# A four-stage decoder block on one core: FFN weights prepared early, experts' products reordered, and scratch for squares with split value products in the grouped attention

## The reference

```python
h = x + L0_xattn(x, mask, ctx, ...)     # 4 batch rows of 256 tokens, width 256;
                                        # keys = 1601 rows of ctx + 256 own; one head of 256
h = h + L0_ffn(h)                       # 32 experts of 96 + 16 chunk experts of 128, top 4 by
                                        # sigmoid gate, weights renormalised
h = h + L1_xattn(h, ctx)                # 16 query heads, 4 key heads of 128, 1601 keys,
                                        # RMS norm of q and k
out = h + L1_ffn(h)                     # BitNet: y = down(rms(silu(gate(q)) * up(q)) quantised)
# L1_ffn: q = clip(round(x * 127 / max|x|), -128, 127)      per token
#         w = clip(round(w / mean|w|), -1, 1) * mean|w|     per matrix: gate, up 1024x256, down 256x1024
```

## Time and profile before

| what | value |
|---|---|
| median of 3 runs | 1772.55 us (1770.74 to 1777.56) |
| profiled execution, its span | 1774.77 us, 1773.0 us |
| PE, busy | 1471.0 us (83%) |
| DVE, busy | 1182.2 us (67%) |
| ACT, busy | 991.8 us (56%) |
| POOL, busy | 561.8 us (32%) |

### The profile page before, as it was taken

The page is one execution under the profiler, slowest core; times in us unless marked ns, Lnnn a source line. Parts: engine busy times, 40 slices in busy tenths (PEclk is TensorE's granted clock), DMA queues, the critical chain, the costliest instruction groups (busy, mean ns, idle before and its releaser), DMA issues. The chain is left out here.

```text
span 1773.0 us, 26328 instructions
## 1 busy us (share of the span) xinstructions
PE 1471.0 (83%) x9411; PEld 1328.1 (75%) x9414; DVE 1182.2 (67%) x2432; ACT 991.8 (56%) x2068; POOL 561.8 (32%) x458
## 2 busy tenths in 40 slices
PE   5787737888847889899999989999989999999835
PEld 4777636787736788888888878888878888888723
DVE  3444367898755776677667667667666766767577
ACT  3333215788624555566556565665656665656455
POOL 2101224454253422334233243232324322322124
PEclk9888957999978999999999999999999999999968
DMA  2011017899711202011010110110201101000020
GB/s 91 32 37 37 19 55 255 295 301 324 237 56 51 51 19 65 19 36 39 7 39 19 53 49 7 39 31 15 65 19 37 39 7 40 19 10 22 21 83 25
DMA packets 80673, 118.19 MB, mean 67 GB/s; under 512 B 16676, under 2 KB 61896, under 8 KB 80552
## 3 DMA queue, kind: packets, MB, share of 16 engines
q1 hardware_dynamic: 75992, 104.14, 18.0%
q0 software_dynamic: 4560, 12.46, 3.1%
HBM read 106.14 MB, written 10.42 MB: 66 GB/s over the span
## 5 line engine op out<-in xcount | busy, mean ns | idle before, releaser
L1617 ACT ACTIVATE ga_pT<-ga_ps_t 128x512 fp32r<-128x512 f32 (+1 forms) x512 | 243.7, 516 | 217.0 <-PE ga_ps_t L1850 216.7
L1747 DVE TENSOR_TENSOR ga_pT<-ga_ps_t,ga_pT 128x512 fp32r<-128x512 f32 (+1 forms) x512 | 278.0, 581 | 46.9 <-ACT ga_pT L1617 45.4
L1625 ACT ACTIVATE ga_probs<-ga_ps_s,ga_neg_max 128x1200 f32<-128x1200 f32 (+1 forms) x256 | 235.4, 927 | 110.6 <-DVE ga_neg_max L1768 110.5
L1850 PE MATMUL ga_ps_t<-all_eye,ga_probs 128*128 128x128 f32 (+1 forms) x1664 | 228.0, 274 | 14.9 <-DVE ga_pT L1747 8.2
L1850 PEld LDWEIGHTS ga_ps_t<-all_eye,ga_probs 128*128 128x128 f32 (+1 forms) x1664 | 194.3, 141 | 29.7 <-DVE ga_pT L1747 10.1
L1763 DVE TENSOR_REDUCE ga_part_max<-ga_ps_s 128x1 f32<-128x1200 f32 x128 | 178.7, 1396 | 10.0 <-PE ga_ps_s L1801 9.4
L1801 PE MATMUL ga_ps_t<-side_w_kv,side_encT 128*128 128x256 f32 (+1 forms) x1170 | 161.2, 287 | 27.6 <-DVE side_kn L1740 22.6
L1801 PEld LDWEIGHTS ga_ps_t<-side_w_kv,side_encT 128*128 128x128 f32 (+1 forms) x1170 | 144.8, 185 | 39.6 <-DVE side_kn L1740 29.2
L1888 PE MATMUL ga_ps_m<-ga_pT,side_v 128*128 128x512 f32 (+1 forms) x416 | 161.0, 423 | 13.7 <-DVE ga_out_n L1781 13.4
L1527 POOL TENSOR_TENSOR ga_oT<-ga_out_n,ga_oT 128x256 fp32r<-128x256 f32 x64 | 47.4, 741 | 352.2 <-ACT ga_oT L1640 352.2
L1801 PE MATMUL ga_ps_s<-side_kT,ga_qT 128*128 128x400 f32 (+1 forms) x768 | 157.1, 354 | 1.9 <-ACT ga_probs L1625 1.6
(11 more groups left out here) (305 smaller groups left out, 3054.5 us busy)
## 6 DMA issues: line engine op xcount, KB each, us to landing
ex_raw<-in_L_ffn_packed SPq DMA_DIRECT2D x63, 704.0 KB
ga_w_raw<-in_L_xattn_Wq SPq DMA_DIRECT2D x16, 512.0 KB
ga_w_raw<-in_L_xattn_Wo SPq DMA_DIRECT2D x16, 512.0 KB, 4.7
ga_inv_rows<-ga_inv_row SPq DMA_DIRECT2D x64, 128.0 KB
mix_y_rows<-ex_y SPq DMA_DIRECT2D x63, 128.0 KB
ca_cache<-in_ctx SPq DMA_DIRECT2D x4, 1536.0 KB
side_enc<-in_ctx_turned SPq DMA_DIRECT2D x12, 512.0 KB, 5.3
side_w_kv_raw<-in_L_xattn_Wk SPq DMA_DIRECT2D x16, 128.0 KB
```

The source lines that it names most:

```text
L1617: nc.scalar.activation(dst(HI), src, ACT.Copy, scale=scale).then_inc(read, 1)
L1625: nc.scalar.activation(dst, src, ACT.Exp, bias=neg_max[:, n % 2:n % 2 + 1], accum_out=half_sum[:, n % 4, k:k + 1]).then_inc(exped, 1)
L1747: nc.vector.tensor_tensor(dst(LO), src, f32(dst(HI)), ALU.subtract).then_inc(empty, 1)
L1850: mm = nc.tensor.transpose(out[0:top, i * P:(i + 1) * P], probs[step % PB][:, tile * P:tile * P + top], eye[:, :])
```

## The change

Six edits:

1. **FFN weights early.** The host lays the three FFN matrices turned (`ffn_turned`, 128 x 3 x 2048). In `cached_attention` SP loads them behind the first cache load, ACT sums absolute values in rounds 0 to 2, and in the last round PE, DVE and ACT make mean, clip and sign. SP stores 1.5 MB of bf16 signs to DRAM and waits for that. `bit_ffn` loads them ready (3 x 0.5 MB), has no preparation left, and takes the token norm in two parts (tiles 0 to 1, then 2 to 7).
2. The loops of `cached_attention` are written out.
3. **Experts:** on PE the gate/up product of block `i-1` stands before the transposes of block `i`; on ACT `silu` before the copy of `xT`; on DVE `a` before the low part of `xT`. Wq of group 0 is loaded here already.
4. **Start of the grouped attention:** Wq's split comes first, its low part on DVE, `norm` comes before `k_eps` on POOL, a one-element `Exp` runs at the start, and the splits of group 1's Wq, Wk/Wv and of Wo move from before step 0 to steps 0, 2 and 4. Group 1's `q` and `qT` jobs move to steps 2, 3 and 5.
5. **Squares** go to `squares_of` (two halves in turn for `kv`, both for `q`).
6. **Value products** of a step are cut into two pieces; the first late job stands between them.

```diff
@@ cached_attention, ACT and DVE, in a round (b < 3, and last)
+                if b < W:
+                    act.wait_ge(f_in, 16 * W)
+                    nc.scalar.activation(f_sign[:, b, :], f_raw[:, b, :], ACT.Abs, accum_out=f_abs[:, b:b + 1]
+                                         ).then_inc(f_summed, 1)
...
+                    for n in range(W):
+                        nc.vector.tensor_scalar(f_raw[:, n, :], f_raw[:, n, :], f_scale[:, n:n + 1], 1.0, ALU.mult, ALU.min
+                                                ).then_inc(f_step, 1)
+                        dve.wait_ge(f_step, n + 3)
+                        nc.vector.tensor_scalar(f_raw[:, n, :], f_raw[:, n, :], -1.0, ROUND, ALU.max, ALU.add
+                                                ).then_inc(f_rounded, 1)
@@ cached_attention, SP
+            sp.wait_ge(f_signed, W)
+            sp.dma_start(ternary.rows, f_sign[:, :, :]).then_inc(f_stored, 16)
+            sp.wait_ge(f_stored, 16)
@@ grouped_attention, the plan
         if to == 1:
-            early, late = [], [e for e in late if e[0] in ("q", "q_eps", "qT")]
+            early, late = [], {2: [("q", 0, 1)], 3: [("q", 1, 1), ("q_eps", 0, 1)],
+                               5: [("qT", 0, 1), ("qT", 1, 1)]}.get(s, [])
...
-        return (([("scores", 0, n)] if n < N else []) + turns[0:2] + early + weighed(n) + late[:1] + turns[2:4]
-                + late[1:])
+        return (([("scores", 0, n)] if n < N else []) + turns[0:2] + early + values[0:1] + late[:1] + values[1:2]
+                + turns[2:4] + late[1:])
@@ grouped_attention, ACT
                 elif kind == "kv":
-
                     at, top, src = kv_view(e)
-                    nc.scalar.activation(kn[0:top, at, :], src[:, :, 0, :], ACT.Square)
-                    nc.scalar.activation(v[g % 2][0:top, HI, at, :], src[:, :, 1, :], ACT.Copy).then_inc(read, 1)
+                    nc.scalar.activation(v[g % 2][0:top, HI, at, :], src[:, :, 1, :], ACT.Copy)
+                    nc.scalar.activation(squares_of[0:top, nth % 2, 0:at.stop - at.start, :], src[:, :, 0, :], ACT.Square
+                                         ).then_inc(read, 1)
...
+            split_q(0)
+            nc.scalar.activation(warm[:, :], half_power[:, 0:1], ACT.Exp)
             for e in prologue:
-                if e[0] == "xT":
-                    split_q(0)
                 if e[0] in RING:
                     ring(e)
-            split_out(0)
-            split_q(1)
-            split_kv(2)
@@ grouped_attention, DVE
+                if kind == "kv":
+                    at, top, src = kv_view(e)
+                    dve.wait_ge(*copied(e))
+                    nc.vector.tensor_copy(kn[0:top, at, :], src[:, :, 0, :])
+                    nc.vector.tensor_tensor(v[g % 2][0:top, LO, at, :], src[:, :, 1, :],
+                                            f32(v[g % 2][0:top, HI, at, :]), ALU.subtract).then_inc(empty, 1)
+                    nc.vector.tensor_reduce(k_sq[0:top, at], squares_of[0:top, nth_squared[e] % 2, 0:at.stop - at.start, :],
+                                            AX.X, ALU.add).then_inc(squares, 1)
+                    return
```

More of the change, by code:

```diff
@@ L160, in cached_attention @@
         added = counted("added", QT, before=1)
+        f_in = sem("f_in")
+        f_summed = sem("f_summed")
+        f_mean = sem("f_mean")
+        f_step = sem("f_step")
+        f_rounded = sem("f_rounded")
+        f_signed = sem("f_signed")
+        f_stored = sem("f_stored")
         block = ctx.enter_context(nc.Block())
         def rounds(eng, body):
-            with eng.Fori(0, B - 1) as b:
-                body(b, False)
-            body(B - 1, True)
+            for b in range(B):
+                body(b, b == B - 1)
         @block.sync
@@ L183, in _ @@
             load_cache(kv_cache[0:1, :, :])
-            with sp.Fori(0, B - 1) as b:
-                row = kv_cache[bass.ds(b + 1, 1), :, :]
+            for n in range(W):
+                sp.dma_start(f_raw[:, n, :], ffn_turned[:, n, :]).then_inc(f_in, 16)
+            for b in range(B - 1):
                 sp.wait_ge(v_lo.sem, v_lo.level(b, 1))
-                load_cache(row)
+                load_cache(kv_cache[b + 1:b + 2, :, :])
+            sp.wait_ge(f_signed, W)
+            sp.dma_start(ternary.rows, f_sign[:, :, :]).then_inc(f_stored, 16)
+            sp.wait_ge(f_stored, 16)
         @block.gpsimd
@@ L256, in body @@
                     move(m)
+                if b < W:
+                    act.wait_ge(f_in, 16 * W)
+                    nc.scalar.activation(f_sign[:, b, :], f_raw[:, b, :], ACT.Abs, accum_out=f_abs[:, b:b + 1]
+                                         ).then_inc(f_summed, 1)
+                if last:
+                    for n in range(W):
+                        act.wait_ge(f_rounded, n + 1)
+                        nc.scalar.activation(f_sign[:, n, :], f_raw[:, n, :], ACT.Copy, bias=-ROUND
+                                             ).then_inc(f_signed, 1)
                 move_hi(ready.level(b, M_TURNS + 1 if last else M), *output)
@@ L456, in body @@
                         turn(m, b + 1)
+                    if last and i == SHARE:
+                        pe.wait_ge(cleared, 4)
+                        pe.wait_ge(f_summed, W)
+                        nc.tensor.matmul(ps_t[:, 0, 0:W], ones[:, :], f_abs[:, :], start=True, stop=True
+                                         ).then_inc(f_mean, 1)
                     n = REST if tile == FULL else P
@@ L860, in _ @@
             for i in range(NBLK + 3):
+                g = i - 1
+                if 0 <= g < NBLK:
+                    act.wait_ge(gu_ready, g + 1)
+                    nc.scalar.activation(silu[g % 2][:, :], ps_g[:, g % 2, 0:GU], ACT.Silu).then_inc(silu_ready, 1)
                 if i < NBLK:
@@ L1224, in weighed @@
         u, half = ((n - 3) // 2, 0) if n % 2 else (n // 2 - 2, 1)
-        return [("weigh", half, u)] if 0 <= u < UNITS else []
+        return [("weigh", (half, piece), u) for piece in range(2)] if 0 <= u < UNITS else []
     def prepared(n):
@@ L1282, in grouped_attention @@
                     read_place[e] = len(read_place)
+    squared = [e for n in range(-1, N + DRAIN) for e in plan[n] if e[0] in ("q", "kv")]
+    nth_squared = {e: n for n, e in enumerate(squared)}
     with ExitStack() as ctx:
@@ L1918, in bit_ffn @@
     W = 3
+    parts = [range(0, 2), range(2, TT)]
     assert DC == 2 and IC == 8 and NB == 2 and TT == 8
@@ L2104, in _ @@
-            for t in range(TT):
-                last_one = nc.vector.tensor_scalar(xn[:, t, :], x_sb[:, t, :], mean_var[:, t, 0:1], rstd[:, t:t + 1],
-                                                   ALU.subtract, ALU.mult)
-            then(last_one)
-            then(nc.vector.tensor_reduce(x_max[:, :], xn[:, :, :], AX.X, ALU.max, apply_absolute_value=True))
-            then(nc.vector.tensor_scalar(x_max[:, :], x_max[:, :], EPS, None, ALU.max))
-            then(nc.vector.reciprocal(x_inv[:, :], x_max[:, :]))
@@ L2139, in gate @@
+            for n in range(len(parts)):
+                norm(n)
             def gate(k):
```

352 lines of the change are left out of this document (181 added, 171 removed).

## The result

The changed kernel takes 1719.59 us, median of four runs, against 1771.64 us (four runs, too): ratio 0.9701, 95% interval 0.9669 to 0.9734. That is 52 us less; 46 were forecast, and the range of 1706 to 1748 held it. Three of the four runs lie between 1718.8 and 1719.9 us; the fourth took 4921.7, which nothing seen here explains and which did not come back in five further runs of the same kernel (1716.6 to 1721.4, median 1719.85, ratio 0.9691, 0.9672 to 0.9710).

What follows compares the result with a forecast made beforehand. PE was taken to bound most of the grouped attention, an engine chain with DMA close behind the experts, latency the FFN's prelude. 1774.8 + 0 + 6 − 12 − 31 − 10 gave 1727.8, 1726 us at the median; 80% within 1706 to 1748.

Steps and rivals of the forecast that it cites:

- the FFN's term: FFN prelude: gate(0) 22.2 us after the first statistics where it was 32.1, 10 us less, range 8 to 11.
- the attention's 31 us: Grouped attention: gain from squares scratch and split value products, summed from 9.2, 17.2 and 4.3 us; bounds 14 and 45.
- Squares: Grouped attention's kv jobs: the scratch lets the bank go 0.33 us earlier, 28 times, 9.2 of 22.6 us.
- Steps 2 and 6: Attention steps with a late kv job: ACT is held by the exponential, so moving the product earlier brings nothing.
- Step 3: Attention step with qT turns behind a kv job: waits fall by 1.23 of 1.32 us, 14 times, 17.2 us.
- Step 7: Attention step whose first late job is a kT: 0.31 us in 14 groups, 4.3 of 14.5 us.
- Steps 0, 1, 4, 5: The other steps of each attention group; the forecast's sum gave them no gain.
- rival E: Attention: value products' second half waits behind a late job's bank; 0.37 us in 128 steps eats 47 us, 0.45 gives 1784; 3%.
- Start: Start of the grouped attention: exponential 11.6 us earlier, step 1's scores 13.5, less 0 to 2.1; 12 us, range 9 to 14.
- FFN weights in the cached attention: Cached attention: sign preparation hidden or at most 1 us late, store waited for at the barrier, +2 us (+1 to +3).
- Loops: Cached attention: written-out loops save loop and address instructions, −2 us for three rounds, bounds 0 and −4.
- Experts: Experts: new order lengthens the chain for two steps from 5.77 to 6.24 us; +6 us, range −3 to +15.

Runs made afterwards that it cites:

- e10: The changed kernel with value products cut only in steps 2 and 6 of each group, whole in all other steps; 1745.9 us in one profiled run.
- e2: The changed kernel with value products whole again and the first late job behind them, the scratch for squares kept; 1745.04 us, ratio 0.9832.
- e5: The changed kernel with the splits of group 1's Wq, Wk/Wv and of Wo before step 0 again; 1726.92 us, ratio 0.9734.
- e7: The changed kernel with the experts' old order, FFN weights loaded behind the second cache load, signs stored in three pieces; 1715.71 us, ratio 0.9669.
- e6: The kernel before the change with only its cached attention loops written out; 1772.89 us, ratio 0.9992.
- e0: The changed kernel run again without edits; 1719.85 us, ratio 0.9691.
- e1: The changed kernel with the experts' old order on PE, ACT and DVE; 1716.67 us, ratio 0.9683.

## Why the prediction was right, point by point

The parts that gained are those forecast, and the FFN's term came out for the reasons given. That the attention's 31 us met 33 is in good part luck: the three terms of that sum measured 7.8, 9.7 and 0, 17.5 in place of 31, and a gain that had no term filled the gap. Nor had the 3.9 us that group 0 gained behind the scores of its step 1.

- **Squares.** "28 × 0.33 = 9.2 us": right in mechanism; alone it measured 7.8, on top of the split 5.2.
- **Steps 2 and 6.** "In this step moving the product earlier brings nothing": right alone (e10 gained nothing). But the `kv` waits fell further than 9.2, from 22.6 to some 8, once all steps were cut. The passage "the exponential stays where it is" failed: it starts 0.5 us earlier in step 2, since DVE's maximum does.
- **Step 3.** 17.2 us forecast. Measured 9.7 for the cut (12.6 of the sum), and of the 0.33 per group from the scratch nothing (e2: 18.5 us of waiting in both). The error is "1.23 of the 1.32": ACT did take the job up early, but the second `qT` turn then waits 0.58 us for a `pT` bank. The prediction asked what is late next, and answered it for the value products only. Two of its signs failed: `qT` waits were to be under 3 us (8.7 measured), and `kT` waits about 10 (5.3).
- **Step 7.** 4.3 us forecast, 0 measured, though the wait itself fell by 10. A smaller wait wasn't a shorter step.
- **Steps 0, 1, 4, 5.** No term in the sum; 15.5 us by the times between exponentials, 10.5 of them in step 1. The forecast missed this altogether, and it made up for steps 3 and 7. No wait of PE pointed to it: in step 1 it shows only as DVE's late maximum.
- **Value products waiting behind the late job**, rival E: its mechanism did appear, in one kind of step. In step 6 the late `kv` job waits for its bank with half of the value products behind it, 8.6 − 3.7 = 4.9 us more than before over 14 groups, 0.35 us each; in e10 6.4. Over 128 steps this and the longer wait for `out_n` (about 3 us) are 0.06 us a step, where 0.37 would have decided. PE's busy time did not grow (1471.0 and 1471.8 us).
- **Start.** −12 forecast, as 11.6 at the exponential and 13.5 at the scores of step 1, less up to 2.1 later. Measured: −10.0 and −12.0, and then no loss but a gain, so that start and group 0 together give −15.9. Group 0, first exponential to first of group 1, ran 5.9 us faster. 2.0 of the 5.9 are the scores of step 1, which no longer stand behind the product of group 1's `q` (3.4 us after the exponential before, 1.4 now). The rest goes with the split of the value products, which works in group 0 too (2.5 us, e2), and the moved splits of the weights (1.7, e5). The sum had counted edits 5 and 6 for 14 groups only.
- **FFN.** 22.2 forecast for the new prelude, 21.9 measured, and 21.8 or 21.9 in all eleven profiles with this edit. The rest of the FFN took 50.4 to 54.4 us in these and 53.9 to 55.5 in the three without the edit, so its −2.3 can't be put down to the change.
- **FFN weights in the cached attention.** The signs were ready for the store at 214.2, not 212.1, and the output at 214.6: both 2 us later, about as much as the first round's projections were slower (5.49 us, not 3.01). The store took 5.1 us for 1536 KB, not 6.8. The estimate from the Trainium skill's page "DMA: Bandwidth & Descriptors", section "Anatomy of one DMA", was 5.6, from figures that the page gives for DMAs issued by GpSimd, while SP issued this one. It is nearer than scaling the 1 MB row by its bytes (7.8), which scales the fixed part too; the 1 MB store itself took 5.2 us. The store's cost, waited for at the barrier, was 0.7 us (e7 takes it back), +2 forecast.
- **Loops.** −2 allowed; −1.4 ± 3 measured over whole runs (e6). Where a gain shows, it is in the routing behind them (last section).
- **Experts.** +6 forecast, +7.3 in the profile, +5 as the mean over all profiles. The chain came out as reckoned, 6.11 against 6.24; and mostly the early steps pay: by ACT's copies of xT a step took 3.06 us in the first 15 and now 3.45 (3.06 to 3.14 in the five profiles with the old order, 3.28 to 3.46 in the nine with the new), 3.32 and 3.35 in the next 15, 3.14 and 3.20 in the rest. ACT's waits for raw weights fell from 21.1 to 15.1 us (16.5 in e0, but 21.2 in e1 with the old order), where the forecast took off 1 to 2.

## What to carry to other kernels

When one engine is busy over 90% of the time and works through a fixed list, it can pay to put a product whose result leaves by way of other engines in the middle of a long run of products that need nothing, not at its end: 25 us here, but all of it in half of the steps. Price such a move by what the other engines' queues do with the earlier product, up to the next step's softmax; summing the waits that the bound engine shows misses what is won there and counts what comes back at another bank. And after reordering a pipeline for one engine, count what the new order puts between two links of the chain on the others: the experts' order here cost that part 5 us, which the attention's gain hid.
